# Counting edge sources by six low bits and 98 high values in place of seven bits and 49

## The chip, the cores and the metric

The kernel runs on one core of one Trainium2 chip. The metric is device time in microseconds (us) of one execution. A time quoted for a kernel is the median of several runs; the profile comes from one further execution, whose own time stands beside it. In the rows, PE is TensorE (PEld its weight loads), DVE is VectorE, ACT is ScalarE, POOL is GpSimd and SP is SyncE.

## What is computed

A graph layer with 6250 nodes of 256 features and 106250 edges, followed by a feed-forward layer with 8 experts of which each node takes two. Only the first part of the graph layer matters for this change: every message is scaled by the root of its source's out-degree, so the sources have to be counted before any message can be gathered.

```python
def _L0_gnn_ref(features, edge_src, edge_dst, W, b):
    ones = jnp.ones(edge_src.shape[0], dtype=features.dtype)
    out_deg = jax.ops.segment_sum(ones, edge_src, num_segments=N_NODES)
    in_deg = jax.ops.segment_sum(ones, edge_dst, num_segments=N_NODES)
    norm_src = jax.lax.rsqrt(jnp.maximum(out_deg, 1.0))
    norm_dst = jax.lax.rsqrt(jnp.maximum(in_deg, 1.0))
    xw = features @ W
    msg = xw[edge_src] * norm_src[edge_src][:, None]
    agg = jax.ops.segment_sum(msg, edge_dst, num_segments=N_NODES)
    h = agg * norm_dst[:, None] + b
    return jax.nn.relu(h)
```

The features that enter are layer-normalised, the result is added to the input, normalised again and sent through the experts (two matrix products with a gelu between them), and added once more.

## The kernel before

The kernel is one program for five engines, each with its own queue of instructions; semaphores order them. It falls into three stretches.

First, the preparation, from the start to some 133 us. SyncE loads sources and destinations as rows of 1024 edges; TensorE turns the sources by transposes so that 104 columns of 8 edges lie on 128 partitions (srcI). VectorE splits each source into its low seven bits and the rest (lohi, L1326 and L1327) and casts both to bf16 (lo16). Then the out-degrees are counted by a product of one-hot tiles. The 832 columns of 128 edges are handled in NCH = 26 chunks of TC = 32 columns. For each chunk VectorE compares lo16 with a constant ramp (irep): ohl is [128 edges, 128 low values, 32 columns], ohh is [128 edges, 49 high values, 32 columns]. TensorE then issues 32 products into one PSUM area of 128 x 49, one for each column j, all in one accumulation over the 26 chunks:

```python
e.tensor_tensor(ohl[i][:, :, :], lo.to_broadcast([128, 128, TC]), irep[:, :, :], ALU.is_equal)
e.tensor_tensor(ohh[i][:, :, :], hi.to_broadcast([128, T, TC]), irep[:, 0:T, :], ALU.is_equal).then_inc(s_oh, 1)
...
for j in range(TC):
    inst = e.matmul(PS[6][:, 0:T], ohl[c % 2][:, :, j], ohh[c % 2][:, :, j],
                    start=(c == 0 and j == 0), stop=(c == NCH - 1 and j == TC - 1))
```

The first operand of a product (ohl) is loaded as weights, the second (ohh) is moved through. Since the column index j is the innermost one of both tiles, an operand's successive elements are 32 elements of two bytes apart. There are two buffers of each tile: VectorE builds chunk c after TensorE has finished chunk c - 2 (s_deg), TensorE starts chunk c when it is built (s_oh). After two chunks VectorE and TensorE put in the check of the edges' order (limits()), after five VectorE reads its result (flags()).

Meanwhile ScalarE loads x, centres its rows and sums their squares (L1053 to L1061), with the means scaled by POOL (L791). POOL had first built the constants (ident, irep, ones and others), counted by s_const.

After the last chunk VectorE takes the root of the variances (rs), waits for the last product (L1345), reads the counts from PSUM (L1346), takes their root (rsqrt, eleven small steps), multiplies it into rs and releases ScalarE and VectorE, which write the scaled rows as two f16 halves (zh, L1067 and L1354, 49 tiles). SyncE stores them to zt. The counts have the layout of the node tiles: partition p, column t is node 128 t + p. VectorE also turns lohi into row numbers of zt (L1357), which needs the seven-bit split.

Behind the last product TensorE does the small products for the experts' constants (L1145, L1147). POOL waits for all of zh (s_zl) and then issues the 832 gathers of messages (L832).

Second, from 133 us to some 1345 us, POOL gathers, TensorE sums the gathered rows by destination (L1165, with one-hot tiles S as weights, read at a step of 8 elements), and the node steps, the expert weights' splitting (L1176 among it) and the experts' products (L1251, L1266) are put between, in an order that a planner wrote out ahead of time. L1222 to L1225 are small products with packed bf16 operands for the routing. Third, the outputs are added up. Neither of these two stretches is touched by the change.

Of the kernel before, what the change touches and what calls it, by code (L numbers as in the profile page):

```python
# [8 lines left out]
T = 49  # L9
NP = T * 128  # L10
# [11 lines left out]
EPS = 1e-5  # L22
EXPONENT = 0x7F800000
TC = 32
NCH = CT * R // TC

ENDS = [10, 17, 24, 31, 36, 41, 45, 49]
# [431 lines left out]
def gnn_ffn(nc, x, src, dst, W, b, Wr, br, ln_g, ln_b, W1, b1, W2, b2, out):  # L459
    f32, f16, bf16 = mybir.dt.float32, mybir.dt.float16, mybir.dt.bfloat16  # L460
    i32, u32 = mybir.dt.int32, mybir.dt.uint32
    ALU = mybir.AluOpType
# [5 lines left out]
    with ctx:  # L468
        def sem(name):
            return ctx.enter_context(nc.semaphore(name))  # L470
# [4 lines left out]
        def sb(name, shape, dt, c=ctx):  # L475
            return c.enter_context(nc.sbuf_tensor(name, shape, dt))
# [16 lines left out]
        ident = sb("ident", [128, 128], f32)  # L493
# [11 lines left out]
        mask = sb("mask", [128, T], f32)  # L505
        far = sb("far", [128, T], f32)
        rs = sb("rs", [128, T], f32)
        tardy = sb("tardy", [R, NGR - 1], f32)
        tok = sb("tok", [128, T], i32)
# [14 lines left out]
        zero = sb("zero", [128, 257], f32)  # L524
        blank = sb("blank", [128, XW], f32)

        PS = [ctx.enter_context(nc.psum_tensor(f"ps{i}", [128, 512], f32)) for i in range(8)]
# [5 lines left out]
        ph = ExitStack()  # L533
        irep = sb("irep", [128, 128, TC], bf16, ph)
# [2 lines left out]
        rows = sb("rows", [E, 12, 128], f32, ph)  # L537
        lohi = sb("lohi", [128, 2, CT * R], i32, ph)
        lo16 = sb("lo16", [128, 2, CT * R], bf16, ph)
        ohl = [sb(f"ohl{i}", [128, 128, TC], bf16, ph) for i in range(2)]  # L540
        ohh = [sb(f"ohh{i}", [128, T, TC], bf16, ph) for i in range(2)]
        sums = sb("sums", [128, T], f32, ph)
        ssq = sb("ssq", [128, T], f32, ph)
        junk = sb("junk", [128, 256], f32, ph)
# [2 lines left out]
        vv = sb("vv", [128, T], f32, ph)  # L547
# [79 lines left out]
        def row(t):  # L627
# [1 line left out]


        CONST = ["ident0", "ident", "irep", "ones", "oneb", "tri", "iota", "area", "room", "gone", "rev", "kio", "pio", "tardy",
                 "tok", "mask0", "mask", "far", "zero", "blank0", "blank"]
        const = {n: i + 1 for i, n in enumerate(CONST)}
        s_const = sem("s_const")
        s_ix0, s_ix1 = sem("s_ix0"), sem("s_ix1")
# [6 lines left out]
        s_src = sem("s_src")  # L642
        s_oh = sem("s_oh")
        s_deg = sem("s_deg")
        s_sum = sem("s_sum")
        s_mean = sem("s_mean")
        s_cen = sem("s_cen")
# [99 lines left out]
        def pool(e):  # L747
            def made(inst):
                inst.then_inc(s_const, 1)

            def count(tile, pattern, base=0, mult=0):
# [5 lines left out]
                                 fill=1.0, base=0, pattern=[[-1, 128]], channel_multiplier=1))  # L757
# [5 lines left out]
                                 fill=0.0, base=0, pattern=[[1, 128]], channel_multiplier=-1))  # L763
# [8 lines left out]
            for g in range(NGR - 1):  # L772
                inst = e.tensor_scalar(tardy[:, g:g + 1], pio[0:R, :], float(AFTER[g]), None, ALU.is_ge)
                if g == NGR - 2:
# [5 lines left out]
                                 fill=0.0, base=N, pattern=[[-128, T]], channel_multiplier=-1))  # L780
# [3 lines left out]
            made(e.memset(blank[:, :], 0.0))  # L784
            e.wait_ge(s_const, const["blank0"])
            made(e.memset(blank[:, 256:257].bitcast(i32), FAR))

            for g in range(7):
                gs = slice(7 * g, 7 * g + 7)
# [63 lines left out]
            for kind, arg in ORDER:  # L853
                if kind == "fetch":
                    fetch(arg)
                elif kind == "xs":
                    c, j = arg
                    e.wait_ge(s_xrow, CHUNKS[c][1])
                    e.wait_ge(s_slot, c + 1)
                    for i in range(2):  # L860
                        e.indirect_dma_start(  # L861
                            out=xs, out_offset=bass.IndirectOffsetOnAxis(ap=slI[:, i, CHUNKS[c][0] + j:CHUNKS[c][0] + j + 1].bitcast(u32), axis=0),
                            in_=xrow[:, OFF[c] + j, :], in_offset=None, bounds_check=SPARE * BS - 1,
                            oob_is_err=False).then_inc(s_sc[n_sent % NSC], 16)
                        n_sent += 1
                elif kind == "cg":
                    t = arg
# [251 lines left out]
        def tensor(e):  # L1119
# [15 lines left out]
            for c in range(NCH):  # L1135
                if c == 2:
                    limits()
                e.wait_ge(s_oh, c + 1)
                for j in range(TC):
                    inst = e.matmul(PS[6][:, 0:T], ohl[c % 2][:, :, j], ohh[c % 2][:, :, j],  # L1140
                                    start=(c == 0 and j == 0), stop=(c == NCH - 1 and j == TC - 1))
                inst.then_inc(s_deg, 1)
            e.wait_ge(s_misc, 16 * 7)
            for k in range(2):
                e.matmul(PS[3][:, 96:96 + E], ones[:, :], Wr_sb[:, k, :], start=(k == 0), stop=(k == 1))  # L1145
# [124 lines left out]
        def vector(e):  # L1270
            made = {"n": 0}

            def then(inst):

                made["n"] += 1
                inst.then_inc(s_chain, 1)
                e.wait_ge(s_chain, made["n"])
# [45 lines left out]
            inst.then_inc(s_src, 1)  # L1323
            e.wait_ge(s_src, 1)
            sv = srcI[:, :, :].rearrange("p c r -> p (c r)")
            e.tensor_scalar(lohi[:, 0, :], sv, 127, None, ALU.bitwise_and)  # L1326
            then(e.tensor_scalar(lohi[:, 1, :], sv, 7, None, ALU.arith_shift_right))  # L1327
            then(e.tensor_copy(lo16[:, :, :], lohi[:, :, :]))
            e.wait_ge(s_const, const["irep"])
            for c in range(NCH):  # L1330
                if c == 2:
                    limits()
                if c == 5:
                    flags()
                i = c % 2
                lo = lo16[:, 0, c * TC:(c + 1) * TC].unsqueeze(1)
                hi = lo16[:, 1, c * TC:(c + 1) * TC].unsqueeze(1)
                if c >= 2:
                    e.wait_ge(s_deg, c - 1)
                e.tensor_tensor(ohl[i][:, :, :], lo.to_broadcast([128, 128, TC]), irep[:, :, :], ALU.is_equal)  # L1340
                e.tensor_tensor(ohh[i][:, :, :], hi.to_broadcast([128, T, TC]), irep[:, 0:T, :], ALU.is_equal).then_inc(s_oh, 1)  # L1341
            e.wait_ge(s_ssq, T)
            then(e.tensor_scalar(vv[:, :], ssq[:, :], 1.0 / D, EPS, ALU.mult, ALU.add))
            rsqrt(vv[:, :], rs[:, :], tmp[:, :])
            e.wait_ge(s_deg, NCH)  # L1345
            then(e.tensor_scalar(vv[:, :], PS[6][:, 0:T], 1.0, None, ALU.max))  # L1346
            rsqrt(vv[:, :], nsrc[:, :], tmp[:, :])
            then(e.tensor_tensor(rs[:, :], rs[:, :], nsrc[:, :], ALU.mult))
            e.tensor_scalar(rs[:, :], rs[:, :], ZS, None, ALU.mult).then_inc(s_scale, 1)
# [387 lines left out]
```

## Time and profile before

| | |
|---|---|
| median of 3 runs | 1662.73 us (1662.26 to 1664.24) |
| the profiled execution's own time | 1661.44 us |
| its span, first to last instruction | 1660.0 us |
| TensorE products, busy | 1192.6 us (72%) |
| POOL, busy | 1116.0 us (67%) |
| VectorE, busy | 952.5 us (57%) |
| ScalarE, busy | 595.0 us (36%) |

Busy time is an average over stretches with different limits, so a stretch is read by itself: the page's 40 slices (41.5 us each) show who is busy there, the chain of waits shows what each step waited for, and the timeline and the groups by line show how long one instruction of a kind takes. Products of TensorE overlap one another, so the time of one product in a row of many is the row's length divided by their number, not the duration that is given for one.

### The profile page before, as it was taken

The numbers are of one execution on the slowest core, as the hardware profiler recorded it, in microseconds if no ns is written. First come the engines' busy times: TensorE is split into PE (matmuls) and PEld (weight loads), VectorE is DVE, ScalarE is ACT, GpSimd is POOL, SyncE is SP. The second block draws the span as 40 slices with busy tenths as digits, with TensorE's granted clock in tenths as the row PEclk, the third lists the DMA queues.
The fourth block names the chain that finished last, engine by engine and source line by source line (L and its number), as shares of the span: only waits on it lengthen the run. The fifth ranks groups of instructions, "written<-read, shape, count | busy, mean of one in ns | idle before, by whom it ended". The sixth has DMA issues, their size and how long they took to land.

```text
span 1660.0 us, 26618 instructions
## 1 busy us (share of the span) xinstructions
PE 1192.6 (72%) x9098; PEld 989.6 (60%) x9098; DVE 952.5 (57%) x2502; ACT 595.0 (36%) x1169; POOL 1116.0 (67%) x1115
## 2 busy tenths in 40 slices
PE   6954565647358645995599659969839858689995
PEld 5954344535146314982488439848728747479984
DVE  8997456656434353656264734764645749466552
ACT  4954011111032004440345025516315335356662
POOL 5006777777777777777777777777777757673333
PEclk9999566666578557996699769979959969799998
DMA  6027866675375447974787469759658578999882
GB/s 187 1 98 266 266 219 203 213 232 179 117 260 163 110 119 261 312 222 129 260 270 253 138 217 316 255 192 305 188 189 292 179 252 265 258 294 305 264 251 51
DMA packets 195546, 354.75 MB, mean 214 GB/s; under 512 B 25572, under 2 KB 93446, under 8 KB 195412
## 3 DMA queue, kind: packets, MB, share of 16 engines
q1 hardware_dynamic: 130120, 205.39, 36.6%
q0 software_dynamic: 58928, 141.26, 29.5%
q10 hardware_dynamic: 6364, 6.40, 1.2%
q8 instruction: 73, 1.20, 0.3%
q14 instruction: 61, 0.50, 0.1%
HBM read 290.80 MB, written 64.07 MB: 214 GB/s over the span
## 4 chain that ended last, share of the span: by engine, by line
PE 35%; DMA 25%; POOL 19%; issue 9%; DVE 8%; ACT 3%; SPq 0%; POOLq 0%; DVEq 0%; ACTq 0%
DMA gt<-zt,srcI 12%; POOL gt L832 9%; PE ps L1251 9%; PE ps L1266 9%; PE ps L1165 8%; DMA out<-gt,toks 6%; POOL xs L861 6%; DMA out<-acc 3%; PE ps L1140 2%; POOL out L891 2%; PE ps L1176 2%; DVE ohl L1340 2%; PE ps L1203 2%; DMA xb<-xs 1%; ACT h L1112 1%
## 5 line engine op out<-in xcount | busy, mean ns | idle before, releaser
L832 POOL DMA_INDIRECT gt<-zt,srcI x832 | 834.1, 1003 | 254.2 <-issue 181.6
L1165 PE MATMUL ps<-gt,S 128*128 128x257 f16 x1664 | 345.7, 331 | 200.3 <-DMA gt<-zt,srcI 198.9
L1165 PEld LDWEIGHTS ps<-gt,S 128*128 128x128 f16 x1664 | 203.5, 152 | 298.2 <-DMA gt<-zt,srcI 282.8
L1251 PE MATMUL ps<-xe,w1b 128*128 128x256 f16 x2688 | 343.2, 282 | 36.0 <-DVE xe L1656 18.9
L1266 PE MATMUL ps<-w2b,hT 128*128 128x256 f16 x2688 | 315.5, 275 | 13.5 <-DVE yb L1688 7.7
L1251 PEld LDWEIGHTS ps<-xe,w1b 128*128 128x128 f16 x2688 | 269.9, 101 | 78.6 <-DVE xe L1656 21.6
L1112 ACT ACTIVATE h<-ps,cb 128x256 f32<-128x256 f32 x448 | 227.1, 557 | 241.4 <-PE ps L1251 236.4
L1662 DVE SCALAR_TENSOR_TENSOR hT<-h,cb,hT 128x512 f16<-128x512 f32 x224 | 167.7, 750 | 237.4 <-ACT hT L1116 236.8
L1266 PEld LDWEIGHTS ps<-w2b,hT 128*128 128x128 f16 x2688 | 264.3, 99 | 47.5 <-issue 15.4
L1116 ACT ACTIVATE hT<-h,cb 128x512 f16<-128x512 f32 x224 | 161.7, 722 | 7.3
L1090 ACT ACTIVATE aT<-ps 128x256 f32<-128x256 f32 x98 | 37.4, 381 | 314.7 <-PE ps L1196 314.6
L1388 DVE TENSOR_TENSOR S<-dlo,S 128x1024 f16<-128x1024 f16 x104 | 71.6, 689 | 102.4 <-PE ps L1165 101.7
L891 POOL DMA_INDIRECT out<-gt,toks x38 | 60.1, 1581 | 92.9 <-DMA out<-gt,toks 64.4
L1100 ACT ACTIVATE xe<-ps 128x512 f16<-128x512 f32 x56 | 32.5, 580 | 244.6 <-PE ps L1235 244.6
L861 POOL DMA_INDIRECT xs<-xrow,slI x98 | 98.4, 1004 | 29.9 <-issue 29.9
L1235 PE MATMUL ps<-ident,xb 128*128 128x128 f32 x224 | 37.9, 296 | 104.0 <-DMA xb<-xs 104.0
L1656 DVE SCALAR_TENSOR_TENSOR xe<-ps,xe 128x512 f16<-128x512 f32 x56 | 38.3, 683 | 120.5 <-ACT xe L1100 120.5
L1534 DVE SCALAR_TENSOR_TENSOR acc<-ps,dhi,acc 128x257 f32 x208 | 91.1, 479 | 22.8 <-PE ps L1165 8.8
L1235 PEld LDWEIGHTS ps<-ident,xb 128*128 128x128 f32 x224 | 28.3, 152 | 107.5 <-DMA xb<-xs 106.7
L1140 PE MATMUL ps<-ohh,ohl 128*128 128x49 bf16 x832 | 84.3, 278 | 9.7 <-DVE ohh L1341 8.9
L1140 PEld LDWEIGHTS ps<-ohh,ohl 128*128 128x128 bf16 x832 | 81.5, 150 | 12.8 <-DVE ohh L1341 12.8
L1176 PE MATMUL ps<-gb,w1b 128*128 128x1 f32 x256 | 52.4, 339 | 34.5 <-DMA w1b<-in_L_ffn_W 34.5
(264 smaller groups left out, 1246.7 us busy)
## 6 DMA issues: line engine op xcount, KB each, us to landing
w1b<-ws SPq DMA_DIRECT2D x56, 1024.0 KB, 6.5
w2b<-ws SPq DMA_DIRECT2D x56, 1024.0 KB, 8.1
ws<-w2b SPq DMA_DIRECT2D x16, 1024.0 KB, 5.0
xb<-xs SPq DMA_DIRECT2D x56, 260.0 KB, 8.3
gt<-zt,srcI POOLq DMA_INDIRECT x832, 4.2
ys<-yb SPq DMA_DIRECT2D x34, 256.0 KB, 7.8
w1b<-in_L_ffn_W SPq DMA_DIRECT2D x8, 1024.0 KB, 8.7
hT<-in_L_ffn_W SPq DMA_DIRECT2D x8, 1024.0 KB, 13.9
```

The source lines that it names most:

```text
L832: e.indirect_dma_start(out=gt[:, i % NG, :], out_offset=None, in_=zt, in_offset=bass.IndirectOffsetOnAxis(ap=srcI[:, c, r:r + 1].bitcast(u ...
L861: e.indirect_dma_start(out=xs, out_offset=bass.IndirectOffsetOnAxis(ap=slI[:, i, CHUNKS[c][0] + j:CHUNKS[c][0] + j + 1].bitcast(u32), axis=0),
L891: e.indirect_dma_start(out=out, out_offset=bass.IndirectOffsetOnAxis(ap=toks[:, a, i:i + 1].bitcast(u32), axis=0), in_=late_rows(a)[:, i, ...
L1112: inst = e.activation(h32[n % NH][:, z, :], UP[n % 2][:, z * BS:(z + 1) * BS], ACT.Gelu, bias=cb[m % 3][:, 2 * q + z:2 * q + z + 1], scale ...
L1116: e.activation(hT[m % 2][:, 0, 2 * q:2 * q + 2, :], h32[n % NH][:, :, :], ACT.Copy, scale=cb[m % 3][:, 9:10]).then_inc(s_hi, 1)
L1140: inst = e.matmul(PS[6][:, 0:T], ohl[c % 2][:, :, j], ohh[c % 2][:, :, j], start=(c == 0 and j == 0), stop=(c == NCH - 1 and j == TC - 1))
L1165: inst = e.matmul(PS[r % 2][:, 0:257], S[:, r % NS, :, c], gt[:, i % NG, part * 257:part * 257 + 257], start=(c == 0 and part == 0), stop= ...
L1176: inst = e.matmul(PV[:, j:j + 1], w3[:, kk, j * 128:(j + 1) * 128], gb[:, ex, 2 + kk:3 + kk], start=(kk == 0), stop=(kk == 1))
L1251: inst = e.matmul(UP[n % 2][:, z * BS:(z + 1) * BS], w[:, l, kk, j * 128:(j + 1) * 128], xe[m % 2][:, k, kk, :], start=(kk == 0 and l == 0 ...
L1266: inst = e.matmul(PY[:, h * D:(h + 1) * D], hT[m % 2][:, k, j, h * 128:(h + 1) * 128], w[:, l, j, :], start=(j == 0 and l == 0 and k == 0) ...
L1534: inst = e.scalar_tensor_tensor(out=a, in0=PS[r % 2][:, 0:257], scalar=dhi[:, w, r:r + 1], in1=a, op0=ALU.mult, op1=ALU.add)
L1662: e.scalar_tensor_tensor(out=hT[m % 2][:, 1, 2 * q:2 * q + 2, :], in0=h32[n % NH][:, :, :], scalar=cb[m % 3][:, 9:10], in1=hT[m % 2][:, 0, ...
```

## The change

The low part of a source now has LO = 64 values (six bits) and the high part HI = NP // LO = 98. The one-hot tiles become [128, 64, 32] and [128, 98, 32], and the products write a PSUM area of 64 x 98. Node 64 h + l lies in partition l and column h there. To bring this to the former layout, VectorE copies the area into SBUF (cnt), and TensorE adds two products: even columns go to partitions 0 to 63 by the identity, odd columns to partitions 64 to 127 by a shifted identity (up64), which POOL makes at the start. VectorE waits for that before it goes on as before, and repeats the seven-bit split of the sources in between, since L1357 needs it.

```diff
+LO = 64
+HI = NP // LO
...
-        ohl = [sb(f"ohl{i}", [128, 128, TC], bf16, ph) for i in range(2)]
-        ohh = [sb(f"ohh{i}", [128, T, TC], bf16, ph) for i in range(2)]
+        ohl = [sb(f"ohl{i}", [128, LO, TC], bf16, ph) for i in range(2)]
+        ohh = [sb(f"ohh{i}", [128, HI, TC], bf16, ph) for i in range(2)]
+        cnt = sb("cnt", [LO, HI], f32, ph)
+        up64 = sb("up64", [LO, 128], f32, ph)
...
+            made(e.memset(up64[:, :], 0.0))
+            e.wait_ge(s_const, const["up0"])
+            made(e.affine_select(out=up64[:, :], in_=up64[:, :], compare_op=ALU.not_equal,
+                                 fill=1.0, base=LO, pattern=[[-1, 128]], channel_multiplier=1))
...
                 for j in range(TC):
-                    inst = e.matmul(PS[6][:, 0:T], ohl[c % 2][:, :, j], ohh[c % 2][:, :, j],
+                    inst = e.matmul(PS[6][0:LO, 0:HI], ohl[c % 2][:, :, j], ohh[c % 2][:, :, j],
                                     start=(c == 0 and j == 0), stop=(c == NCH - 1 and j == TC - 1))
                 inst.then_inc(s_deg, 1)
+
+            e.wait_ge(s_const, const["up64"])
+            e.wait_ge(s_cnt, 1)
+            for z, at in enumerate((ident[0:LO, :], up64[:, :])):
+                inst = e.matmul(PS[6][:, 128:128 + T], at, cnt[:, :].rearrange("p (t z) -> p t z", z=2)[:, :, z], start=(z == 0), stop=(z == 1))
+            inst.then_inc(s_deg, 1)
...
-            e.tensor_scalar(lohi[:, 0, :], sv, 127, None, ALU.bitwise_and)
-            then(e.tensor_scalar(lohi[:, 1, :], sv, 7, None, ALU.arith_shift_right))
+            e.tensor_scalar(lohi[:, 0, :], sv, LO - 1, None, ALU.bitwise_and)
+            then(e.tensor_scalar(lohi[:, 1, :], sv, 6, None, ALU.arith_shift_right))
             then(e.tensor_copy(lo16[:, :, :], lohi[:, :, :]))
...
-                e.tensor_tensor(ohl[i][:, :, :], lo.to_broadcast([128, 128, TC]), irep[:, :, :], ALU.is_equal)
-                e.tensor_tensor(ohh[i][:, :, :], hi.to_broadcast([128, T, TC]), irep[:, 0:T, :], ALU.is_equal).then_inc(s_oh, 1)
+                e.tensor_tensor(ohl[i][:, :, :], lo.to_broadcast([128, LO, TC]), irep[:, 0:LO, :], ALU.is_equal)
+                e.tensor_tensor(ohh[i][:, :, :], hi.to_broadcast([128, HI, TC]), irep[:, 0:HI, :], ALU.is_equal).then_inc(s_oh, 1)
...
             e.wait_ge(s_deg, NCH)
-            then(e.tensor_scalar(vv[:, :], PS[6][:, 0:T], 1.0, None, ALU.max))
+            e.tensor_copy(cnt[:, :], PS[6][0:LO, 0:HI]).then_inc(s_cnt, 1)
+            e.tensor_scalar(lohi[:, 0, :], sv, 127, None, ALU.bitwise_and)
+            then(e.tensor_scalar(lohi[:, 1, :], sv, 7, None, ALU.arith_shift_right))
+            e.wait_ge(s_deg, NCH + 1)
+            then(e.tensor_scalar(vv[:, :], PS[6][:, 128:128 + T], 1.0, None, ALU.max))
             rsqrt(vv[:, :], nsrc[:, :], tmp[:, :])
```

## Rows read from the trace of the kernel before

**Rows 1.** The page's 40 slices: VectorE's busy tenths and TensorE's granted clock.

```profile
DVE  8997456656434353656264734764645749466552
PEclk9999566666578557996699769979959969799998
```

**Rows 2.** The chain of waits, 0 to 260 us: start, length, what.

```profile
56.23 3.43 PE ps L1140 x32
...
102.66 3.35 PE ps L1140 x32
...
110.02 19.64 DVE zh L1354 x49
...
133.20 1.20 POOL gt L832
```

**Rows 3.** Timelines of ScalarE and POOL, 0 to 110 us: start, length, instruction, idle before.

```profile
91.02 0.19 ACT L1061 ACTIVATION_READ_ACCUMULATOR junk<-acc 128x1 f32 x1
...
27.63 1.54 POOL L791 TENSOR_SCALAR sums<-sums 128x7 f32<-128x7 f32 x1 [6.42 <-ACT acc L1053]
```

**Rows 4.** Timeline of VectorE, 0 to 140 us.

```profile
10.59 0.59 DVE L1327 TENSOR_SCALAR lohi<-srcI 128x832 int32<-128x832 int32 x1
...
12.28 2.29 DVE L1340 TENSOR_TENSOR ohl<-lo,irep 128x4096 bf16<-128x4096 bf16 x1
14.49 0.97 DVE L1341 TENSOR_TENSOR ohh<-lo,irep 128x1568 bf16<-128x1568 bf16 x1
15.38 2.28 DVE L1340 TENSOR_TENSOR ohl<-lo,irep 128x4096 bf16<-128x4096 bf16 x1
...
102.53 0.18 DVE L1343 TENSOR_SCALAR vv<-ssq 128x49 f32<-128x49 f32 x1
...
106.10 0.21 DVE L1346 TENSOR_SCALAR vv<-ps 128x49 f32<-128x49 f32 x1 [0.73 <-PE ps L1140]
```

**Rows 5.** Timeline of TensorE's products, 0 to 60 us.

```profile
15.52 6.43 PE L1140 MATMUL ps<-ohh,ohl 128*128 128x49 bf16 x64 [7.02 <-DVE ohh L1341]
22.92 0.76 PE L1123 MATMUL ps<-dg,ones 104*128 104x104 f32 x2 [0.97 <-DVE lim L1301]
...
23.80 1.63 PE L1127 MATMUL ps<-ident,idf 104*128 104x104 f32 x8
```

**Rows 6.** Line L1140: duration min/median/max in ns; who waited for it.

```profile
L1140 PEld LDWEIGHTS ps<-ohh,ohl x832: 136/149/180, 15.5 to 105.6; 128*128 128x128 bf16 x167
L1140 PE MATMUL ps<-ohh,ohl x832: 262/280/310, 15.5 to 105.7; 128*128 128x49 bf16 x167
...
  DVE ohl L1340: 3.6, 11
```

**Rows 7.** Timeline of TensorE's products, three stretches.

```profile
105.82 0.96 PE L1145 MATMUL ps<-Wr_sb,ones 128*128 128x8 f32 x4
...
196.84 6.83 PE L1176 MATMUL ps<-gb,w1b 128*128 128x1 f32 x32
...
422.26 0.46 PE L1222 MATMUL ps<-Mb,oneb 128*128 128x8 bf16 x10
```

**Rows 8.** Busy time by stretch; the granted clock stands after POOL.

```profile
990.00:1080.00 90.00, 86.60 (x775) 77.99 (x774) 55.90 (x150) 49.65 (x90) 69.35 (x68) 1.00 0.87 289
398.00:478.00 80.00, 32.37 (x139) 18.74 (x138) 33.15 (x122) 4.77 (x9) 61.11 (x63) 0.50 0.52 167
```

**Rows 9.** Weight loads by line and shape, 990 to 1080 us: busy, mean ns.

```profile
L1251 PEld LDWEIGHTS ps<-xe,w1b 128*128 128x128 f16 x297 | 28.9, 98 | 4.6 <-DVE xe L1656 1.5
...
L1165 PEld LDWEIGHTS ps<-gt,S 128*128 128x128 f16 x147 | 17.7, 146 | 3.4 <-DMA gt<-zt,srcI 2.9
```

**Rows 10.** Products by line and shape, 398 to 478 us: busy, mean ns.

```profile
L1222 PE MATMUL ps<-Mb,oneb 128*128 128x8 bf16 x10 | 0.5, 173 | 0.0
...
L1225 PE MATMUL ps<-Mb,oneb 128*128 128x48 bf16 x1 | 0.2, 222 | 0.0
```

More of the change, by code:

```diff
@@ L631, in gnn_ffn @@
         CONST = ["ident0", "ident", "irep", "ones", "oneb", "tri", "iota", "area", "room", "gone", "rev", "kio", "pio", "tardy",
-                 "tok", "mask0", "mask", "far", "zero", "blank0", "blank"]
+                 "tok", "mask0", "mask", "far", "zero", "blank0", "blank", "up0", "up64"]
         const = {n: i + 1 for i, n in enumerate(CONST)}
@@ L644, in gnn_ffn @@
         s_deg = sem("s_deg")
+        s_cnt = sem("s_cnt")
         s_sum = sem("s_sum")
```

## Prediction

> **What bounds the kernel now.** I read the page's slices first [rows 1]. The change sits in the first 110 us of a span of 1660.0 us, where VectorE stands at 8 or 9 tenths. Next I read the chain of waits in that stretch [rows 2]. It alternates: VectorE builds a pair of one-hot tiles (L1340, L1341), TensorE runs 32 products on it (L1140), VectorE waits for that buffer and builds the next pair. The last products end at 106.01, VectorE reads the counts at 106.10 [rows 4] and takes the root, and then 49 steps of zh and POOL's first gather at 133.20 follow one another with nothing else late. No transfer or engine has work that could be done before that gather, so whatever the count stage gains or loses moves everything behind it by the same amount. POOL's and ScalarE's early work isn't on this chain: ScalarE's last sum of squares ends at 91.2, 15 us ahead of its reader, and POOL idles for 6.4 us before 27.63 [rows 3].
>
> So the question is who sets the pace of the 26 chunks. On VectorE a chunk is 2.21 us from the start of ohl to the start of ohh and 0.89 us from there to the next ohl, 3.10 us [rows 4]. On TensorE 64 products back to back took 6.43 us, of which 0.18 is the end of the last one (0.28 long, the next starts 0.10 after it), so 98 ns per product and 3.13 us per chunk [rows 5, 6]. VectorE waits for TensorE 11 times, 3.6 us in all [rows 6], at every second chunk. The two paces are within 2%: shortening one of them alone gives little, lengthening either one is paid in full, 26 times.
>
> **Part by part: VectorE.** Elements per partition and chunk go from 4096 + 1568 to 2048 + 3136. The two intervals above give (2.21 - 0.89) / 2528 = 0.522 ns per element and 0.07 us per instruction. The new pair is 1.14 + 1.71 = 2.85 us against 3.10: 0.25 us per chunk, 6.5 us over 26. The first pair lets TensorE start 0.25 us sooner.
>
> **Part by part: TensorE.** There are still 832 products. Each loses half its weight columns (ohl, 128 to 64) and doubles its moving columns (ohh, 49 to 98). Both operands are read at a step of 32 elements, 64 bytes, because TC is the innermost index. What sets the 98 ns decides everything, and three comparisons bear on it.
>
> First, neither the issue nor a weight load of 128 16-bit columns takes that long. At granted clock 0.50 [rows 8], L1222 loads 128 packed columns each time and moves 8; ten such products take 0.46 us with the last one's 0.17, or 32 ns each [rows 7, 10]. The stage of the change is at the same lower level of 1.2 GHz, though the page's line has 9 there: the four passes of L1145 right behind the last count took 0.96 us, or 240 ns each with the last one's end, much like the 213 ns a pass of L1176 (6.83 us for 32) at 196.84, in a slice that the page gives as 5 [rows 1, 7].
>
> Second, a load at a step is dearer, but not dear enough. L1165 reads its weights at a step of 16 bytes; its loads take 146 ns where the packed ones of L1251 take 98 in the same stretch, 48 more [rows 8, 9]. L1140's load takes 149 (median) [rows 6]. 32 + 48 = 80 ns is the most I can make of the load, below 98, and loads overlap the running product (L1165 keeps its pace behind 257 moving columns).
>
> Third, the moving side fits. A product with 48 packed moving columns takes 222 ns at the lower clock (L1225) [rows 10]; L1140, with 49 at a step, takes 280 [rows 6]. The excess is 58 ns. 49 packed columns are 41 ns at 1.2 GHz, and 41 + 58 = 99 ns, the spacing just found. So I take the moving operand at a step as the bound, 98 / 49 = 2.0 ns per column, and 98 columns at 196 ns per product, 6.27 us per chunk. VectorE's 2.85 us then lies wholly beside it. No row shows 98 moving columns at a step. Bounds: the shortest L1140 (262) gives 262 - 222 + 41 = 81 ns or 1.65 per column, 162 ns per product; the slowest chunk of the chain (3.43 us, or 107 ns a product) gives 214 [rows 2].
>
> The stage after: first product at 15.52 - 0.25 = 15.27; 832 x 0.196 = 163.1; the products of limits() no longer fall into an idle gap and cost the 2.5 us that they took from 22.92 to 25.43 [rows 5]; 0.2 for the last end. That is 181.1, and VectorE reads 0.1 later at 181.2 instead of 106.10: +75.1 us. With the bounds: +46.8 and +90.0.
>
> **Part by part: bringing the counts over.** On the chain now stand the copy of 64x98 out of PSUM (0.25 to 0.3; L1346's 128x49 took 0.21), two f32 products in two passes each (0.96, as the four passes of L1145) and a hand-over of 0.1 each way (last product's end 106.01 to 106.10): 1.4 us [rows 2, 4, 7]. The two repeated lohi steps (0.59 or less each) run on VectorE between copy and answer, 0.25 + 1.15 = 1.4, so they are covered, just; without that cover they cost 1.1. Bounds 1.2 to 2.5. On TensorE the new wait holds back L1145 and L1147, 2 us of work for gb, which VectorE reads (L1374) only behind the 49 zh steps, 20 us later [rows 2]; nothing waits. POOL's memset and select for up64, two short steps on one tile, fall into its 6.4 us of idle time [rows 3]. ssq's root steps, before the last wait, get 6 us of cover instead of none.
>
> Sum: 75.1 + 1.4 = +76.5 us. Against the profiled execution's own 1661.44 that is 1737.9; the median of the three runs shown, 1662.73, is 1.3 higher, so **1739 us**. With the bounds, 1711 to 1755.
>
> **The rivals.**
> *The weight load sets the spacing (faster).* If 98 ns is the load of 128 columns at a step, then 64 columns free TensorE: 98 packed-rate moving columns need 82 ns, 2.6 us per chunk, below VectorE's 2.85. VectorE then sets the pace. From 12.28 to 102.53 it now spends 26 x 3.10 = 80.6 on pairs and 3.6 on TensorE, so 6.0 on limits(), flags() and hand-overs; 12.28 + 26 x 2.85 + 6.0 = 92.4, just behind ScalarE's 91.2. Then come 2.8 us of root steps (102.53 to 105.37) and 1.4 for the hand-over [rows 3, 4, 6]: 96.6 against 106.10, so 1653 us. It decides if the stepped load takes over 82 ns and the stepped column under 0.9. For it: the spacing of 98 ns is near to 128 columns at one per cycle of 1.2 GHz. Against it: the 80 ns above, and the 58 ns by which the product itself is longer. A spacing shared by all 177 columns (0.55 ns each, 162 now: 90 ns) lands beside it, near 1655. Together 0.09.
> By the Trainium skill, page "TensorE: Matmul & The Clock Gate", section "LDWEIGHTS (loading the stationary operand)", a load's nanoseconds are its column count divided by 1.2, whatever the depth: 107 for 128 columns and 53 for 64, which would give this rival; the 32 ns of L1222 speak against it for packed 16-bit weights.
>
> *The halved load is the slower load.* If 64 columns are read one by one at 2.0 ns, 128 ns, and this doesn't overlap the product, a product takes 324 ns: 269.6 us in place of 163.1, 1845 us. Against it: the 32-bit loads of L1176 (213 ns a pass) overlap, and a stepped load hides behind L1165's products. 0.05.
> The same page, section "Weight-path perf modes", has a fast load only for exactly 128 non-FP32 columns, so this change would lose it; no row shows a 16-bit load of 64, and at 128 ns it still lies under 196.
>
> *The clock.* If twice the columns lift the clock to 2.4 GHz and the stepped column halves with it, TensorE keeps about 98 ns and the time stays at about 1663. Against it: a stepped load is 48 ns above a packed one even at granted 1.00 [rows 8, 9], and the share of streaming in each product is what it was. 0.03.
>
> **How the numbers follow.** Forecast with its bounds 0.80, faster rival 0.09, doubled load 0.05, clock 0.03, other delays 0.03. The forecast's own bounds leave out 2 in 10 and no more, so they are the range, 1711 to 1755. A difference of 0.2% (3.3 us) is about what can be told from no change. Faster 0.09, same 0.03, slower 0.88.
>
> **What would show it.** In the profile after: L1140's line at some 196 ns a product, VectorE's idle time before ohl some 3.4 us per chunk and ended by TensorE, VectorE's pair at 2.8 us, counts read near 181, first gather near 210, all later stages as long as now. Wrong if TensorE idles before the products (VectorE sets the pace), if the spacing stays near 98, or if it passes 214.

## The result: 58 us slower, and the profile after

The changed kernel takes 1722.34 us (median, 1717.33 to 1725.79) where the kernel before, beside it on the same chip, takes 1664.05: a ratio of 1.0341, with a 95% interval of 1.0322 to 1.0359, or 53.6 to 59.7 us more. The prediction was 1739 us, 1711 to 1755: the right sign and cause, 17 us too much. The profiled execution of after spans 1720.6 us against 1660.0.

The lines of the code have moved: the counting product is L1150 now, the one-hot tiles are L1356 and L1357, the copy of the counts is L1362, the two products behind it L1157, the answer L1366, zh L1374 and the gather L842.

The page's slices of after first, VectorE's busy tenths and TensorE's granted clock, against [rows 1]. A slice is 43 us long here.

```profile
DVE  6555755666643434455445563583554738466552
PEclk9999955665657865899589958998968979799998
```

VectorE falls from 8 or 9 tenths to 5 or 6 in the first slices, and the stage lasts into the fourth. It is no longer VectorE that works without a pause. The chain of waits from the start (start, length, what) names who does, against [rows 2]:

```profile
15.27 11.19 PE ps L1150 x64
...
28.89 131.55 PE ps L1150 x768
160.52 0.26 DVE cnt L1362
160.92 1.07 PE ps L1157 x4
162.09 0.22 DVE vv L1366
...
166.01 19.64 DVE zh L1374 x49
189.15 1.20 POOL gt L842
```

Before, the chain alternated between the two engines, chunk by chunk; now one run of 768 products holds it for 131.55 us. The counts are read at 160.52 where they were read at 106.10 [rows 4]. zh begins 55.99 us later than in [rows 2], and so does the first gather (189.15 - 133.20 = 55.95).

TensorE's timeline over the same stretch (start, length, instruction, idle time before), against [rows 5, 7]:

```profile
15.27 11.19 PE L1150 MATMUL ps<-ohh,ohl 128*64 128x98 bf16 x64 [6.77 <-DVE ohh L1357]
26.38 0.76 PE L1133 MATMUL ps<-dg,ones 104*128 104x104 f32 x2
...
28.82 1.45 PE L1150 MATMUL ps<-ohh,ohl 128*64 128x98 bf16 x7
...
161.91 1.03 PE L1161 MATMUL ps<-Wr_sb,ones 128*128 128x8 f32 x4
```

Sixty-four products took 6.43 us before and take 11.19 now. The long run gives the spacing: 131.55 / 768 = 171 ns a product, against 98. The products of limits() start the moment the 64 are done, with no idle time before them, so they stand in the chain. The last line, four f32 passes, took 0.96 us before and takes 1.03 now; in four64 below, the same passes take 0.61 us at granted clock 1.00. So the stage ends at the lower of the two clock levels (1.2 GHz) in both kernels, though the page's slices have a 9 there.

The product's own view (duration min/median/max; then who waited for it, in us and times), against [rows 6], and VectorE's timeline at the first pair, at one chunk and at the end of the stage:

```profile
L1150 PEld LDWEIGHTS ps<-ohh,ohl x832: 185/194/203, 15.3 to 159.9; 128*64 128x64 bf16 x167
L1150 PE MATMUL ps<-ohh,ohl x832: 343/350/416, 15.3 to 160.1; 128*64 128x98 bf16 x167
...
  DVE ohl L1356: 59.2, 23
  DVE cnt L1362: 5.3, 1
```

```profile
12.29 1.23 DVE L1356 TENSOR_TENSOR ohl<-lo,irep 128x2048 bf16<-128x2048 bf16 x1
13.43 1.78 DVE L1357 TENSOR_TENSOR ohh<-lo,irep 128x3136 bf16<-128x3136 bf16 x1
15.13 1.22 DVE L1356 TENSOR_TENSOR ohl<-lo,irep 128x2048 bf16<-128x2048 bf16 x1
...
45.56 1.23 DVE L1356 TENSOR_TENSOR ohl<-lo,irep 128x2048 bf16<-128x2048 bf16 x1 [2.52 <-PE ps L1150]
...
160.52 0.25 DVE L1362 COPY cnt<-ps 64x98 f32<-64x98 f32 x1 [5.31 <-PE ps L1150]
```

VectorE waits for TensorE 59.2 us where it waited 3.6: at 23 of 26 chunks, 2.52 us in the one shown.

### The profile page after: what moved, and what is told of

Same layout as the page of the kernel before. It is cut to its first block, busy times and chain, and to the rows that moved or that the text cites. A ratio compares the mean times of both kernels' runs of the same rounds, so it can differ in the third digit from the quotient of the medians.

```text
span 1720.6 us, 26634 instructions
## 1 busy us (share of the span) xinstructions
PE 1255.4 (73%) x9102; PEld 1051.1 (61%) x9102; DVE 949.1 (55%) x2505; ACT 593.9 (35%) x1169; POOL 1118.7 (65%) x1117
## 4 chain that ended last, share of the span: by engine, by line
PE 39%; DMA 22%; POOL 19%; issue 9%; DVE 6%; ACT 3%; SPq 0%; POOLq 0%; DVEq 0%; ACTq 0%
DMA gt<-zt,srcI 11%; POOL gt L842 9%; PE ps L1282 8%; PE ps L1150 8%; PE ps L1267 8%; PE ps L1181 8%; POOL xs L871 5%; DMA out<-gt,toks 5%; DMA out<-acc 3%; PE ps L1192 2%; POOL out L901 2%; PE ps L1219 2%; ACT h L1122 1%; POOL S L890 1%; DVE zh L1374 1%
## 5 line engine op out<-in xcount | busy, mean ns | idle before, releaser
L842 POOL DMA_INDIRECT gt<-zt,srcI x832 | 837.1, 1006 | 254.1 <-issue 181.6
L1267 PE MATMUL ps<-xe,w1b 128*128 128x256 f16 x2688 | 342.3, 281 | 34.2 <-DVE xe L1676 20.7
L1150 PE MATMUL ps<-ohh,ohl 128*64 128x98 bf16 x832 | 142.8, 348 | 6.8 <-DVE ohh L1357 6.8
L1150 PEld LDWEIGHTS ps<-ohh,ohl 128*64 128x64 bf16 x832 | 142.2, 192 | 7.3 <-DVE ohh L1357 7.1
L1554 DVE SCALAR_TENSOR_TENSOR acc<-ps,dhi,acc 128x257 f32 x208 | 91.2, 480 | 22.3 <-PE ps L1181 9.2
L1251 PEld LDWEIGHTS ps<-ident,xb 128*128 128x128 f32 x224 | 28.8, 154 | 103.4 <-DMA xb<-xs 102.6
```

Source lines behind the costliest of these rows:

```text
L842: e.indirect_dma_start(out=gt[:, i % NG, :], out_offset=None, in_=zt, in_offset=bass.IndirectOffsetOnAxis(ap=srcI[:, c, r:r + 1].bitcast(u ...
L1150: inst = e.matmul(PS[6][0:LO, 0:HI], ohl[c % 2][:, :, j], ohh[c % 2][:, :, j], start=(c == 0 and j == 0), stop=(c == NCH - 1 and j == TC - 1))
L1267: inst = e.matmul(UP[n % 2][:, z * BS:(z + 1) * BS], w[:, l, kk, j * 128:(j + 1) * 128], xe[m % 2][:, k, kk, :], start=(kk == 0 and l == 0 ...
L1554: inst = e.scalar_tensor_tensor(out=a, in0=PS[r % 2][:, 0:257], scalar=dhi[:, w, r:r + 1], in1=a, op0=ALU.mult, op1=ALU.add)
```

## The experiments

Each run is compared with the kernel before on its own chip, since the three chips differ: the kernel before took 1921.63 us beside the first four runs below, 1663.90 beside the three in the middle and 1943.08 beside the last two. On the slower chips the stretch of gathers is longer: 187.7 to 1601.7 us in delay, 133.2 to 1336.8 in the profile of before. The first three runs are single executions, and only their stage is read. Spacings are a group's length by its number of products; where a group is a single short run, its last product's extra length is taken off first.

### l64_move: how the product grows with its moving columns, behind 64 weight columns

The changed kernel, in which the product moves only the first MOVE[c] of the 98 columns. The rest of the counts is left out.

```diff
+MOVE = [HI] * 5 + [80] * 3 + [64] * 3 + [49] * 3 + [32] * 3 + [16] * 3 + [8] * 3 + [HI] * 3
...
-inst = e.matmul(PS[6][0:LO, 0:HI], ohl[c % 2][:, :, j], ohh[c % 2][:, :, j],
+inst = e.matmul(PS[6][0:LO, 0:MOVE[c]], ohl[c % 2][:, :, j], ohh[c % 2][:, 0:MOVE[c], j],
```

> The changed kernel, but chunk by chunk only the first 98, 80, 64, 49, 32, 16 or 8 of the 98 moving columns are multiplied (columns left out are not counted, so the sums of work differ by design); the weights stay 64 columns, both operands stay at a step of 64 bytes, VectorE's tiles stay whole. Read the spacing of the 32 products in a chunk. Theory 1, the moving operand's step sets it (two cycles of 1.2 GHz, 1.67 ns, a column, plus 2.5 and a little for the load): 171 ns at 98, 141 at 80, 114 at 64, 89 at 49 unless a floor by the load (at most 64 x 1.67 = 107) shows first, and below that floor no further fall. Theory 2, the weight load sets it: 171 at every width. Theory 3, a fixed 25 ns and 1.49 a column (the line through 98 ns before and 171 after): 171, 144, 120, 98, 73, 49, 37.

TensorE's groups by shape, 28.8 to 128.8 us (busy us, mean ns of one | idle time before):

```profile
L1151 PE MATMUL ps<-ohh,ohl 128*64 128x80 bf16 x96 | 13.7, 317 | 0.0
L1151 PE MATMUL ps<-ohh,ohl 128*64 128x64 bf16 x96 | 11.2, 291 | 0.0
L1151 PE MATMUL ps<-ohh,ohl 128*64 128x49 bf16 x96 | 11.0, 289 | 0.0
...
L1151 PE MATMUL ps<-ohh,ohl 128*64 128x8 bf16 x96 | 10.7, 253 | 0.0
```

No group has idle time, so busy time is pace: 96 products at 80 columns in 13.7 us are 141 ns each (less some 2 ns for the last end), at 64 columns 115, at 49 and fewer 112 to 110. With 171 at 98 columns, the slope from 64 to 98 columns is (171 - 115) / 34 = 1.65 ns per column. Below 64 columns the moving side no longer decides: something takes 110 ns whatever is moved, and the load of 64 columns is all that stays the same. So the load has a price of its own near 110 ns, and lies hidden below 171; that this price hangs on the weights' step is shown under steps. The kernel took 1939.87 us.

### l128_move: the same behind 128 weight columns

The kernel before, with ohh widened to 98 high values (those over 48 never occur) and the moving columns stepped in the same way. Where fewer than 49 are moved, a part of the counts is left out.

```diff
+HI = 98
+MOVE = [HI] * 5 + [80] * 3 + [64] * 3 + [T] * 3 + [32] * 3 + [16] * 3 + [8] * 3 + [HI] * 3
...
-ohh = [sb(f"ohh{i}", [128, T, TC], bf16, ph) for i in range(2)]
+ohh = [sb(f"ohh{i}", [128, HI, TC], bf16, ph) for i in range(2)]
...
-inst = e.matmul(PS[6][:, 0:T], ohl[c % 2][:, :, j], ohh[c % 2][:, :, j],
+inst = e.matmul(PS[6][:, 0:MOVE[c]], ohl[c % 2][:, :, j], ohh[c % 2][:, 0:MOVE[c], j],
...
-e.tensor_tensor(ohh[i][:, :, :], hi.to_broadcast([128, T, TC]), irep[:, 0:T, :], ALU.is_equal).then_inc(s_oh, 1)
+e.tensor_tensor(ohh[i][:, :, :], hi.to_broadcast([128, HI, TC]), irep[:, 0:HI, :], ALU.is_equal).then_inc(s_oh, 1)
```

> The kernel before with its 128 weight columns, but the high tile widened to 98 values (the upper 49 are all zero) and the products moving 98, 80, 64, 49, 32, 16 or 8 of them chunk by chunk (chunks with fewer than 49 leave counts out). Theory 1: at 98 moving columns 166 plus what the 128-column load adds (14 ns as before, or 5 as after), 171 to 180, at 49 the 98 ns of before, at 32 some 60 to 70, then a floor by the load of 128 at 30 to 80. Theory 2: 98 at every width. Theory 3: 171, 144, 120, 98, 73, 49, 37. Against the run with 64 weight columns it tells at the same 98 moving columns what halving the weights is worth: theory 1 under 10 ns, theory 2 about 73 ns.

The timeline's last three chunks, at 98 columns, then the groups by shape, 10 to 140 us:

```profile
121.01 17.43 PE L1142 MATMUL ps<-ohh,ohl 128*128 128x98 bf16 x96 [1.68 <-DVE ohh L1343]
```

```profile
L1142 PE MATMUL ps<-ohh,ohl 128*128 128x80 bf16 x96 | 14.6, 330 | 0.0
L1142 PE MATMUL ps<-ohh,ohl 128*128 128x64 bf16 x96 | 12.2, 303 | 0.1
L1142 PE MATMUL ps<-ohh,ohl 128*128 128x49 bf16 x96 | 10.1, 280 | 1.3 <-DVE ohh L1343 1.3
...
L1142 PE MATMUL ps<-ohh,ohl 128*128 128x8 bf16 x96 | 6.6, 208 | 5.1 <-DVE ohh L1343 5.1
```

The run of 17.43 us, less its last end, gives 180 ns at 98 columns. The groups at 80, 64 and 49, less the longer end of the last product of each of their chunks, give 150, 125 and 99. The slope is again (180 - 99) / 49 = 1.65 ns per column, and 49 x 1.65 = 81 leaves 17 to 18 ns that don't grow. Behind 64 weight columns the same line gives 171 - 98 x 1.65 = 9 to 10. So the halved weights do save something: 8 to 9 ns a product. The forecast's 196 exceeds the 171 by these two terms: it doubled the 18 along with the columns, and it gave the lighter load nothing.

The floor at 8 columns is (6.6 - 0.4) / 96, some 64 ns, with 128 weight columns (0.4 for the last ends of the three chunks), and 110 with 64. Half the weights take longer to load, at a step of 64 bytes and at the lower clock of this stage. The kernel took 1950.95 us.

The Trainium skill, page "TensorE: Matmul & The Clock Gate", section "Weight-path perf modes", has a fast load only where the number of weights is 128 and they aren't FP32; the two floors, 64 and 110 ns, agree with it, though no row shows which way a load took. The same page's section "LDWEIGHTS (loading the stationary operand)" gives a load as its columns divided by 1.2, 53 ns for 64: here, at a step of 64 bytes, the measurement is 110, and it decides.

### steps: whose step is it, the weights' or the moving operand's

The changed kernel with the one-hot tiles laid out in groups of q columns of edges, so that q is the step in elements (2 bytes each). Each chunk has a q for the weights (qw) and one for the moving operand (qm).

```diff
+STEPS = [(32, 32)] * 2 + [(16, 16)] * 3 + [(8, 8)] * 3 + [(4, 4)] * 4 + [(2, 2)] * 4 + [(32, 4)] * 4 + [(4, 32)] * 3 + [(32, 32)] * 3
+def stepped(tile, n, q):
+    return tile[:, :, :].rearrange("p v j -> p (v j)").rearrange("p (g v q) -> p g v q", v=n, q=q)
...
+qw, qm = STEPS[c]
+inst = e.matmul(PS[6][0:LO, 0:HI], stepped(ohl[c % 2], LO, qw)[:, j // qw, :, j % qw],
+                stepped(ohh[c % 2], HI, qm)[:, j // qm, :, j % qm],
...
+for half, (tile, n) in enumerate(((ohl[i], LO), (ohh[i], HI))):
+    q = STEPS[c][half]
+    v = lo16[:, half, c * TC:(c + 1) * TC].rearrange("p (g q) -> p g q", q=q).unsqueeze(2)
+    inst = e.tensor_tensor(stepped(tile, n, q), v.to_broadcast([128, TC // q, n, q]),
+                           irep[:, 0:n, 0:q].unsqueeze(1).to_broadcast([128, TC // q, n, q]), ALU.is_equal)
```

> The changed kernel with its 64 weight and 98 moving columns, the one-hot tiles laid out chunk by chunk with 32, 16, 8, 4 or 2 of the 32 edge columns innermost, so an operand's step is 64, 32, 16, 8 or 4 bytes; in seven chunks the two operands differ (weights 64 bytes and moving 8, weights 8 and moving 64). Same counts. Theory 1: 171 at 64, 32 and 16 bytes for both, 82 to 90 from 8 bytes on; weights 64 with moving 8: 82 to 107; weights 8 with moving 64: 166 to 171. Theory 2: weights 64 with moving 8 stays at 171, weights 8 with moving 64 falls below 100. VectorE's pair stays at 2.85 us if its pace does not depend on the innermost run, else up to twice that at 4 and 2.

Busy time of the product in seven stretches (stretch, length, busy, number, granted clock, DMA): steps of 32 bytes, 16 bytes, 8 bytes, 4 bytes twice, then weights 64 and moving 8 bytes, then weights 8 and moving 64 bytes.

```profile
28.83:46.16 17.33, 17.33 (x96) 1.00 0.02 5
46.16:63.15 16.99, 16.99 (x98) 1.00 0.00 1
63.15:75.30 12.15, 11.88 (x129) 1.00 0.01 2
77.14:78.80 1.66, 1.66 (x32) 1.00 0.00 0
86.29:89.10 2.81, 2.81 (x32) 0.50 0.02 6
93.65:108.00 14.35, 14.35 (x128) 0.59 0.01 2
108.03:124.00 15.97, 15.97 (x98) 0.50 0.01 1
```

At 32 and 16 bytes the spacing is 180 and 177 ns (96 products each), close to the 171 at 64. At 8 bytes it halves: 11.88 / 129 is 92 ns, 0.9 per column. At 4 bytes it is 47 ns in one chunk and 82 in another, and the granted clock beside them is 1.00 and 0.50: there the spacing follows the clock. The last two lines settle whose step it is. Weights at 64 bytes and moving columns at 8: 14.35 / 128 = 112 ns, the floor in l64_move; with the weights at 8 bytes too it was 92, so that floor belongs to the weights' step. Weights at 8 bytes and moving columns at 64: 167 ns (96 products), as if nothing had been done. So the moving operand's step sets the 171 ns, and the rival by which the weight load sets the spacing falls. The granted clock of 1.00 in the first lines is no sign of the higher level by itself: [rows 1] has a 9 there too, over passes at the lower pace [rows 7].

VectorE pays nothing for the finer layout down to q = 4. Its pairs at 8 bytes and at 4 bytes in the timeline:

```profile
69.47 1.23 DVE L1365 TENSOR_TENSOR ohl<-lo,irep 128x2048 bf16<-128x2048 bf16 x1 [0.30 <-PE ps L1157]
70.61 1.78 DVE L1365 TENSOR_TENSOR ohh<-lo,irep 128x3136 bf16<-128x3136 bf16 x1
...
76.99 1.97 DVE L1365 TENSOR_TENSOR ohl<-lo,irep 128x2048 bf16<-128x2048 bf16 x1
78.85 2.83 DVE L1365 TENSOR_TENSOR ohh<-lo,irep 128x3136 bf16<-128x3136 bf16 x1
```

At q = 4 the pair is as long as in the changed kernel; at q = 2 it goes from 2.85 to 4.6 us. The kernel took 1946.03 us.

The Trainium skill, page "SBUF — State Buffer", section "Specifications (TRN2)", has lines of 16 bytes and asks for two hits in a line for full bandwidth. The trace agrees in part: 2-byte elements 16 to 64 bytes apart cost nearly the same (171 to 180 ns), and at 8 bytes, two to a line, half; but at granted clock 1.00 two to a line are not yet the full rate, since 4 bytes take 47 ns there.

### delay: is the later gather the whole of the loss

The kernel before, with 24 products more in each chunk, into a PSUM area that nobody reads: the count stage is made longer in another way, with the old tiles.

```diff
 for j in range(TC):
     inst = e.matmul(PS[6][:, 0:T], ohl[c % 2][:, :, j], ohh[c % 2][:, :, j],
                     start=(c == 0 and j == 0), stop=(c == NCH - 1 and j == TC - 1))
+for j in range(24):
+    inst = e.matmul(PS[7][:, 0:T], ohl[c % 2][:, :, j], ohh[c % 2][:, :, j], start=True, stop=True)
```

> The kernel before with 24 more products per chunk, into PSUM that nobody reads, so that the count stage lasts about as long as after the change while nothing else of the change is there. If the stage's length is all, the counts are read at 160 to 161 and the whole is longer by the same 54 to 55 us, 1718 to 1719. If something behind the gather answers to the later start, or to the change's other parts, it differs from the shift of the first gather by over 3 us (the changed kernel's first gather is 56.0 later and its span 60.6 longer).

The time is 1972.16 us, a ratio of 1.0264 (1.0202 to 1.0326), or 50.5 us more (38.8 to 62.6). The gathers' line (duration min/median/max, first and last start):

```profile
L832 POOL DMA_INDIRECT gt<-zt,srcI x832: 940/946/2972, 187.7 to 1601.7; - x167
```

The first gather starts 54.5 us later than before, and 54.5 lies in the interval. A kernel that has nothing of the change but its delay loses what the change loses, within the 12 us that this run leaves open to either side; the 3 us that the expectation asked for can't be told from it. The next run narrows it.

### after_again: the changed kernel beside the next two

> The changed kernel as it is, beside the other two on one chip: counts read at 160.5, first gather 56 us later than before, whole 56 to 60 us longer. If the total moves by the gather's shift alone, the ratio answers to 56 us; a larger one says that something behind the gather answers too.

1719.5 us, a ratio of 1.0337 (1.0316 to 1.0359), or 56.1 us more (52.6 to 59.7); the gather is 56.0 later, at 189.2 us. The total moves by the gather's shift, within some 4 us.

### four64: the six-bit split with the operands 8 bytes apart

The changed kernel with q = 4 (INNER) in both tiles throughout.

```diff
+INNER = 4
+def stepped(tile, n):
+    return tile[:, :, :].rearrange("p v j -> p (v j)").rearrange("p (g v q) -> p g v q", v=n, q=INNER)
...
-inst = e.matmul(PS[6][0:LO, 0:HI], ohl[c % 2][:, :, j], ohh[c % 2][:, :, j],
+inst = e.matmul(PS[6][0:LO, 0:HI], stepped(ohl[c % 2], LO)[:, j // INNER, :, j % INNER], stepped(ohh[c % 2], HI)[:, j // INNER, :, j % INNER],
...
+v = lo16[:, half, c * TC:(c + 1) * TC].rearrange("p (g q) -> p g q", q=INNER).unsqueeze(2)
+inst = e.tensor_tensor(stepped(tile, n), v.to_broadcast([128, TC // INNER, n, INNER]),
+                       irep[:, 0:n, 0:INNER].unsqueeze(1).to_broadcast([128, TC // INNER, n, INNER]), ALU.is_equal)
```

> The changed kernel (64 by 98) with four edge columns innermost in both one-hot tiles, so that operands are read at a step of 8 bytes in place of 64; nothing else. If the step is the cause (theory 1), products are 90 ns apart (32 in 2.9 us), VectorE's pair stays at 2.85 us, the counts are read at 96 to 101 us in place of 160.5, and the whole is 4 to 9 us shorter than the kernel before and some 62 us shorter than the changed one. If the loss lay elsewhere in the change, the counts are still read near 160.

TensorE's timeline, then VectorE's:

```profile
15.26 5.97 PE L1156 MATMUL ps<-ohh,ohl 128*64 128x98 bf16 x64 [6.77 <-DVE ohh L1362]
...
34.97 64.16 PE L1156 MATMUL ps<-ohh,ohl 128*64 128x98 bf16 x672 [0.44 <-DVE ohh L1362]
...
100.18 0.61 PE L1167 MATMUL ps<-Wr_sb,ones 128*128 128x8 f32 x4
```

```profile
93.06 1.23 DVE L1362 TENSOR_TENSOR ohl<-lo,irep 128x2048 bf16<-128x2048 bf16 x1 [0.30 <-PE ps L1156]
94.20 1.78 DVE L1362 TENSOR_TENSOR ohh<-lo,irep 128x3136 bf16<-128x3136 bf16 x1
...
99.23 0.25 DVE L1369 COPY cnt<-ps 64x98 f32<-64x98 f32 x1 [0.49 <-PE ps L1156]
```

The first 64 products take 5.97 us in place of 11.19, 90.5 ns each with the last one's end taken off, and the counts are read at 99.23 in place of 160.52. The time is 1661.59 us, a ratio of 0.9976 (0.9955 to 0.9997): 4.0 us less than before (0.5 to 7.5). The whole loss of the change is undone by the order of the elements alone, with its 98 moving columns, its copy and its two small products all in place.

The last line of TensorE's timeline asks for one more reading. The four f32 passes behind the stage take 0.61 us here and 1.03 in the changed kernel: TensorE is at the higher clock level now, so the halving could be the clock's and not the step's. It isn't. Two chunks of 32 products at either level (stretch, length, busy, number, granted clock, DMA) take the same time, 2.89 us:

```profile
25.36:28.25 2.89, 2.89 (x32) 0.50 0.45 138
41.08:43.97 2.89, 2.89 (x32) 1.00 0.00 0
```

### four128: the seven-bit split with the operands 8 bytes apart

The kernel before with the same layout (q = 4, the diff as above). It should tell what the layout is worth without the change.

> The kernel before (128 by 49) with four edge columns innermost in both tiles; nothing else. Products at most 65 ns apart, so VectorE alone sets the pace with 3.10 us a chunk; counts read at 100 to 102 in place of 106.1, the whole 3 to 6 us shorter. If the six-bit split has any worth of its own once the step is gone, the run with 64 by 98 is shorter than this one by 1 to 4 us; if not, the two agree.

1694.01 us, a ratio of 1.0174 (1.0154 to 1.0193): 29.0 us slower. The expectation missed. The products did become faster, as TensorE's timeline shows, and the time went elsewhere, as those of POOL and ScalarE do:

```profile
97.69 1.75 PE L1146 MATMUL ps<-ohh,ohl 128*128 128x49 bf16 x32 [1.35 <-DVE ohh L1346]
```

```profile
41.89 0.28 POOL L797 TENSOR_SCALAR sums<-sums 128x7 f32<-128x7 f32 x1 [9.43 <-ACT acc L1059]
51.30 46.65 POOL L797 TENSOR_SCALAR sums<-sums 128x7 f32<-128x7 f32 x2 [9.13 <-ACT acc L1059]
```

```profile
97.77 0.51 ACT L1063 ACTIVATE acc<-acc,sums 128x256 f32<-128x256 f32 x1 [37.13 <-POOL sums L797]
...
129.60 0.19 ACT L1067 ACTIVATION_READ_ACCUMULATOR junk<-acc 128x1 f32 x1
```

The last 32 products take 1.75 us, 49 ns each, and TensorE now waits 1.35 us per chunk for VectorE, which works without a pause. POOL's step on the means, a 128x7 multiplication of 0.28 us, starts at 51.30. The line holds two of them: the second is short and right behind the first, and both are through only at 97.95, just after VectorE's last pair. ScalarE stands still for 37.13 us of that, and its last sum of squares ends at 129.8 in place of 91.2 [rows 3]. That is the last thing that zh waits for: zh starts at 136.63. In the kernel before the same POOL steps took 0.24 to 2.2 us, and VectorE paused there at every second chunk [rows 6]; in four64, which pauses too, 0.3 to 2.3.

The trace of steps shows the same in the six-bit kernel. VectorE's tiles are slower to build at 4 bytes, and from 72.35 to 96.43 us it doesn't pause:

```profile
76.61 19.92 POOL L807 TENSOR_SCALAR sums<-sums 128x7 f32<-128x7 f32 x1 [9.04 <-ACT acc L1069]
```

The step ends at 96.53, in VectorE's first pause. A step isn't always held off, though: the one at 41.89 above, and one at 80.02 in l128_move, took 0.28 and 0.29 us with no pause of VectorE near them. Both started within 0.11 us before VectorE went from one instruction to the next. What lets a step in between two instructions stays open.

The Trainium skill, page "SBUF — State Buffer", section "🔬 SBUF: two separate sides", has one pair of ports for VectorE and GpSimd, held for a whole instruction by the one that comes first. That POOL's step is held off agrees; but the run has it held off for 46 us, over some thirty VectorE instructions one right behind the other, and not for one.

### four128_act and four64_act: the same two without POOL's step

To test that reading, POOL's step is taken out: ScalarE's own accumulation gives -x/256 at once, into a scratch tile.

```diff
-e.tensor_scalar(sums[:, gs], sums[:, gs], -1.0 / D, None, ALU.mult).then_inc(s_mean, 1)
...
-e.activation(row(t), row(t), ACT.Copy, accum_out=sums[:, t:t + 1]).then_inc(s_sum, 1)
+if t:
+    e.wait_ge(s_sum, t)
+e.activation(junk2[:, :], row(t), ACT.Copy, scale=-1.0 / D, accum_out=sums[:, t:t + 1]).then_inc(s_sum, 1)
...
-e.wait_ge(s_mean, g)
+e.wait_ge(s_sum, 7 * g)
```

> The 128 by 49 kernel with the 8-byte step, and the means no longer scaled by POOL: ScalarE sums x times -1/256 itself (into a tile that nobody reads), so the small POOL step that took 46.65 us in the run before falls away. If VectorE's pauses were what that POOL step needed, and ScalarE waited for it, then ScalarE's sums of squares end near 91 in place of 130, counts are read at 101 to 103, the first gather starts near 128 to 130, and the whole is 3 to 6 us shorter than the kernel before. If the 30 us lost had another cause (the products' closer spacing, the layout), most of them stay.

> The same edit on the 64 by 98 kernel with the 8-byte step. There POOL's steps took 0.3 to 2.3 us, off the chain, so the whole is the same as without the edit within 2 us: 4 to 6 us shorter than the kernel before.

four128_act takes 1937.26 us against 1943.08, a ratio of 0.9974 (0.9954 to 0.9995): 5.1 us less than before (1.0 to 8.9), where four128 was 29.0 more. ScalarE's timeline and the chain:

```profile
96.61 0.19 ACT L1066 ACTIVATION_READ_ACCUMULATOR junk<-acc 128x1 f32 x1
```

```profile
97.64 0.11 DVE vv L1349
...
104.36 19.67 DVE zh L1360 x49
```

ScalarE ends at 96.8 instead of 129.8 (91 was expected; each sum now waits for the one before it), and zh starts at 104.36, 5.7 us earlier than in [rows 2]. So the 29 us were POOL's held-off step. four64_act takes 1939.40 us, a ratio of 0.9982 (0.9962 to 1.0002): 3.5 us less, an interval that includes no change. Its zh starts at 105.07, against 104.44 in four64. The two splits can't be told apart by time once the layout is right: neither 64 by 98 nor 128 by 49 has an advantage of its own that these runs show.

## Why the prediction was right, and where it was too high

**That TensorE would set the pace.** Right. VectorE waits 59.2 us for L1150, the chain runs through 768 products in a piece, and delay shows that the kernel's end follows the later gather.

**VectorE's pair.** Right. 1.14 + 1.70 = 2.84 us from start to start; the forecast was 2.85. The first product starts at 15.27, as forecast.

**The moving operand at a step is the bound.** Right, and shown by steps: with the weights' step cut to 8 bytes the spacing stays at 167 ns, with the moving operand's cut it falls to 112.

**The spacing of 196 ns.** This is the step that failed, in size. It came from 98 / 49 = 2.0 ns for each column, as if every nanosecond of the spacing belonged to a column. l128_move shows that the 98 ns are 49 x 1.65 and 17 to 18 that don't grow, and l64_move that these become 9 to 10 behind half the weights. 98 x 1.65 + 9.5 is 171. So the agreement of 41 + 58 = 99 with the spacing of 98 was in part luck, and so was the lower bound: its 162 was read from the shortest L1140, which happened to give 1.65 per column, and left out the part that doesn't grow. 832 x 25 ns is some 20.7 us, and that is the miss in the stage: the counts were read at 160.5, not 181.2. The time is off by 17 and not by 20.7, as the time of before beside it was 1.3 us longer and the rest lies within the interval. One row at a second number of columns would have split the 98; the trace of before had none.

**limits() without its gap.** Right: from 26.38 to 28.82 is 2.4 us; 2.5 was forecast.

**Bringing the counts over.** From 160.52 to 162.09 is 1.57 us; 1.4 was forecast, within its bounds of 1.2 to 2.5. VectorE's two lohi steps lie inside, as said.

**Everything behind is only shifted.** Right within the interval: the gather is 55.95 later, and the time 53.6 to 59.7 more.

**The rivals.** The rival by which the weight load sets the spacing fell to steps. The 80 ns allowed at most for the load of 128 columns held (the floor is 64 in l128_move). The rival of the slower half was half right: 64 columns do take longer than 128, 110 ns where it supposed 128, but this overlaps the running product, since 171 ns is not the sum of 110 and 162. It is a floor close beneath: in the stretch of steps with the weights at 64 bytes and the moving operand at 8, it sets the pace. The clock rival is out for this kernel: the f32 passes behind the stage took 1.03 us, no less than the 0.96 before, and 0.61 at the higher level. The clock did rise in four64, whose moving operand is 8 bytes apart; there the spacing was 90.5 ns at either level.

**Not settled.** No run has a moving operand 64 bytes apart at a clock that is shown to be the higher one, so it stays open whether the 1.65 ns would change with it.

## What to carry to other kernels

Split the spacing of small products into a part per moving column, a part per weight load and a rest before scaling it: two numbers of columns are enough, and one shape alone can't tell them apart. Look at how far apart the elements of a moving operand lie: here 8 bytes in place of 64 halved the spacing, with VectorE's work unchanged, and turned 56 us of loss into a gain of 4 (0.5 to 7.5). That gain is the layout's and not the split's: the seven-bit split with the same layout, and with POOL's step out of the way, gains 5 (1.0 to 8.9). And when an engine loses its pauses, look at who lived on them: a 0.28 us step on POOL became 46 us, and cost 29 us of the whole.

## What the runs showed of the hardware

- Behind products with 8 moving columns, the spacing has a floor of 110 ns for a weight load of 64 columns at a step of 64 bytes (l64_move) and of 64 ns for one of 128 columns at the same step (l128_move), both at the lower clock.
- A product with 98 moving columns behind 64 weight columns takes 171 ns at a step of 64 bytes, 180 at 32, 177 at 16 and 90.5 at 8; at 8 bytes it is the same at granted clock 0.50 and 1.00. At 4 bytes it follows the granted clock: 47 ns at 1.00 and 82 at 0.50. At 64 bytes one moving column more costs 1.65 ns, behind 64 weight columns (l64_move) and behind 128 (l128_move).
- In the changed kernel, 131.6 us of products at a step of 64 bytes without a pause were followed by f32 passes at the lower level (1.03 us); in four64, at 8 bytes, by passes at the higher one (0.61 us). In four128, at 8 bytes but with 1.3 us of idle time in every chunk, they took 1.00 us again, so the step isn't shown to decide the level by itself.
- VectorE's instructions one behind the other held a small POOL instruction off for 46.4 us (four128) and 19.9 (steps), until VectorE paused; with a pause of 0.3 us at every second chunk the same step took at most 2.3.
